# Pacing 2400 indirect DMAs on POOL: groups of eight behind a held no-op instead of groups of four with drains

## The reference, cut to what matters

```python
src = jnp.concatenate([edge_index[0], loops])
dst = jnp.concatenate([edge_index[1], loops])
e = jax.nn.leaky_relu(a_src[src] + a_dst[dst], negative_slope=0.2)
e_max = jax.ops.segment_max(e, dst, num_segments=M)
ee = jnp.exp(e - e_max[dst])
denom = jax.ops.segment_sum(ee, dst, num_segments=M)
alpha = ee / (denom[dst] + 1e-16)
msg = h[src] * alpha[:, :, None]
agg = jax.ops.segment_sum(msg, dst, num_segments=M).reshape(M, HEADS * NUM_EXPERTS) + b_gat
```

## Time and profile before

| what | us |
|---|---|
| median of 3 runs | 4237.11 |
| span of the profiled execution | 5018.1 |
| POOL busy in it | 2431.5 |
| DVE busy | 2254.2 |
| PE busy (matmul) | 2170.6 |
| ACT busy | 1178.5 |

### The profile page before, as it was taken

One profiled execution on the slowest core, in us unless ns is written; L12 is line 12 of the kernel. 1 busy time (PEld: TensorE's weight loads), 2 busy tenths in 40 slices (PEclk: granted clock), 3 DMA queues, 4 the chain that ended last, 5 costly groups with the idle time before them and its releaser, 6 DMA issues.

```text
span 5018.1 us, 28173 instructions
## 1 busy us (share of the span) xinstructions
PE 2170.6 (43%) x7631; PEld 912.4 (18%) x7631; DVE 2254.2 (45%) x3946; ACT 1178.5 (23%) x1734; POOL 2431.5 (48%) x2473
## 2 busy tenths in 40 slices
PE   0611278885456465556553143436564322000015
PEld 0211133332122121212111011112222111000014
DVE  8899867763336263635346531315140102101235
ACT  0300145552223232323222121224243312000001
POOL 0000162656653626161636666662636554777562
PEclk9955589987677676777766576678686656555557
DMA  3200044432223222322313221212122212011124
GB/s 87 39 1 0 21 73 76 74 71 46 37 52 65 37 61 46 64 41 46 61 19 68 35 49 28 56 34 63 41 68 55 64 34 87 10 24 22 31 47 145
DMA packets 652065, 247.84 MB, mean 49 GB/s; under 512 B 552276, under 2 KB 632708, under 8 KB 649476
## 3 DMA queue, kind: packets, MB, share of 16 engines
q1 hardware_dynamic: 573988, 216.76, 18.3%
q0 software_dynamic: 77920, 29.29, 5.8%
HBM read 152.68 MB, written 91.71 MB: 49 GB/s over the span
## 4 chain that ended last, share of the span: by engine, by line
PE 23%; another core or an unknown queue 20%; DVE 19%; issue 16%; POOL 8%; DVEq 7%; ACT 5%; DMA 2%; SPq 1%; ACTq 0%; POOLq 0%
POOL ring L790 8%; DVE res L1298 4%; PE ps L887 4%; DVEq L1300 4%; PE ps L877 2%; PE ps L991 2%; PE ps L902 2%; PE ps L1002 2%; PE ps L1013 1%; DVE res L1633 1%; DMA arena<-xnT 1%; PE ps L1052 1%; DVE arena L1659 1%; PE ps L950 1%
## 5 line engine op out<-in xcount | busy, mean ns | idle before, releaser
L790 POOL DMA_INDIRECT ring<-table,src_i x2048 | 2004.7, 979 | 1587.0 <-issue 883.0
L887 PE MATMUL ps<-arena,w 64*128 64x448 f32 x896 | 293.8, 740 | 441.5 <-issue 197.9
L754 POOL DMA_INDIRECT ring<-keys_d,place x128 | 138.8, 1084 | 653.8 <-DVEq L1255 589.5
L991 PE MATMUL ps<-arena 64*128 64x512 f32 x800 | 238.5, 710 | 360.2 <-DMA arena<-xnT 221.6
L1013 PE MATMUL ps<-ident,arena 128*128 128x128 f32 x800 | 156.1, 354 | 466.4 <-issue 272.7
L1805 DVE TENSOR_TENSOR arena<-ps,arena 128x1024 f32<-128x1024 f32 x68 | 83.3, 1225 | 594.9 <-remote 410.8
L902 PE MATMUL ps<-arena,w 128*64 128x448 f32 x896 | 247.7, 683 | 237.3 <-issue 237.3
L1645 DVE TENSOR_TENSOR arena<-arena,ps 128x448 f32<-128x448 f32 x297 | 174.8, 618 | 364.9 <-issue 195.7
L1186 ACT ACTIVATE arena<-ps,arena 128x1024 f32<-128x1024 f32 x200 | 217.0, 1115 | 256.6 <-remote 120.3
L1659 DVE TENSOR_TENSOR_SCAN arena<-ps,carry,arena 128x448 f32<-128x448 f32 x122 | 130.8, 1131 | 320.6 <-issue 178.0
L1105 ACT ACTIVATE ps<-ps,tb 128x448 f32<-128x448 f32 x297 | 171.9, 605 | 359.7 <-PE ps L887 154.9
(11 more groups left out here) (338 smaller groups left out, 3968.8 us busy)
## 6 DMA issues: line engine op xcount, KB each, us to landing
arena<-in_x SPq DMA_DIRECT2D x304, 110.0 KB
ring<-table,src_i POOLq DMA_INDIRECT x2048
partial<-res SPq DMA_DIRECT2D x15, 1536.0 KB
arena<-in_x SPq DMA_DIRECT2D x160, 140.0 KB
outputs_d<-arena SPq DMA_DIRECT2D x32, 512.0 KB
arena<-outputs_d SPq DMA_DIRECT2D x32, 512.0 KB
arena<-xnT SPq DMA_DIRECT2D x100, 128.0 KB
arena<-h_tok SPq DMA_DIRECT2D x50, 256.0 KB
```

The lines of the kernel that those rows point to most:

```text
L790: g.indirect_dma_start(out=ring[k % 2][:, j - FROM[k], :], out_offset=None, in_=table[0:GRAPH_NODES, :], in_offset=off(ap=src_i[:, j:j + 1 ...
L887: mm(bank(1 + (2 * i + z) % 3)[:, 0:CHUNK], w2[lower_upper(z), i * P:(i + 1) * P], h1[lower_upper(z), :], start=True, stop=True).then_inc( ...
L991: m = mm(hid[ee % 2][:, z * NT:(z + 1) * NT], fw1[lower_upper(z), ee, :], xf[q][lower_upper(z), :], start=True, stop=True)
```

## The change

`GROUP` becomes 8 and the drains go. The wait of each group is put on a no-op of its own that is not merged with the instruction behind it (`nofuse`), so that POOL's sequencer stands at it, and it waits for the group just in front, all eight, instead of the group two in front. It applies to the search, the scatters, all 2048 gathers and the nodes.

```diff
-GROUP = 4
-BURST = 16
-BURSTS_UNTIL = 1536
+GROUP = 8
...
-            def rest(n):
-
-                if n % BURST == BURST - 1 and n < BURSTS_UNTIL:
-                    g.drain()
+            def hold(done, value):
+
+                pool.wait_ge(done, value)
+                g.nop(nofuse=True)
 
             def group_landed(done, n):
 
-                if n % GROUP == 0 and n >= 2 * GROUP:
-                    m = n // GROUP
-                    pool.wait_ge(done[m % 2], 16 * GROUP * (m // 2))
-                return done[n // GROUP % 2]
+                m = n // GROUP
+                if n % GROUP == 0 and m:
+                    hold(done[1 - m % 2], 16 * GROUP * ((m + 1) // 2))
+                return done[m % 2]
 
             def node_group(n, j):
 
                 half = j // GROUP % 2
-                if j % GROUP == 0:
-                    of = n if j - 2 * GROUP >= NODE_BATCHES[n][0] else n - 1
-                    if of >= 0:
-                        pool.wait_ge(nrows[of % 2][half], node_count(of, half, j - GROUP))
+                if j % GROUP == 0 and j:
+                    of = n if j - GROUP >= NODE_BATCHES[n][0] else n - 1
+                    hold(nrows[of % 2][1 - half], node_count(of, 1 - half, j))
                 return nrows[n % 2][half]
 
             def gather_group(k, i):
 
-                half = i // GROUP % 2
-                if i % GROUP == 0 and i >= 2 * GROUP:
-                    pool.wait_ge(gath[k % 2][half], (gathered(k) - 16 * SIZES[k]) // 2 + 16 * (i // GROUP // 2 * GROUP))
-                elif i % GROUP == 0 and k:
-                    pool.wait_ge(gath[1 - k % 2][half], gathered(k - 1) // 2)
-                return gath[k % 2][half]
+                m = i // GROUP
+                if i % GROUP == 0 and i:
+                    hold(gath[k % 2][1 - m % 2], (gathered(k) - 16 * SIZES[k]) // 2 + 16 * GROUP * ((m + 1) // 2))
+                elif i == 0 and k:
+                    hold(gath[1 - k % 2][1], gathered(k - 1) // 2)
+                return gath[k % 2][m % 2]
...
             for k in range(P):
-                rest(k)
                 done = group_landed(search, k)
```

More of the change, by code:

```diff
@@ L771, in _ @@
                 for k in TILES_AFTER[j]:
-                    rest(n)
                     scatter(k, group_landed(scattered, n))
@@ L787, in _ @@
                 for j in range(FROM[k], FROM[k] + SIZES[k]):
-                    rest(j)
                     done = gather_group(k, j - FROM[k])
```

## The result

The changed kernel takes 4619.69 us (median of 4 runs, 4617.70 to 4623.08), the kernel before 4238.16 us beside it: 1.0895 times as long, with an interval of 1.0879 to 1.091. The forecast was 4356 us, the range ended at 4450 us. The sign is right and the size is not: +382 us instead of +119.

A forecast was written before the change was run, and what follows sets the result against it. It took the bound to change from stage to stage, with POOL's gathers setting the time from chunk 6 on. Its terms, 70 + 20 + 24 + 23 - 18 = +119 us, on 4237 gave 4356 us; range 4140 to 4450.

The forecast's parts named there:

- One hold: POOL standing at the no-op until the eight DMAs in front have landed: 1.5 us each, range 1.1 to 2.5.
- The end, chunks 13 to 16: Last gathers, with no drains to remove: 47 holds that count, at 1.5 us, +70 us (52 to 118).
- Chunk 12: Gathers of the chunk that had no drains: 16 holds, +24 us (18 to 40), counted for the timed runs.
- Chunks 6 to 11: Gathers taken as back to back: each loses 8 drains and gains 16 holds, together +23 us (-16 to +121).
- Chunks 0 to 5: First gathers: +3.8 us a chunk, taken as hidden by the waits for buffers, so nothing in the sum.
- Nodes: 128 gathers of nodes with 15 holds, 13 of them counted at 1.5 us: +20 us (0 to 33).
- Search and scatters: POOL's other DMAs: two holds' worth of cost each, taken as hidden, so nothing in the sum.
- Relief for PE: Front and experts: pauses twice as often halve the wait of PE's late semaphores, -18 us (-25 to 0).
- The faster rival: PE's late semaphores are in the timed runs and more frequent pauses relieve them: 4188 or 4118 us; chance 0.25.
- Only the end counts: POOL still waits for buffers in the middle, so chunks 6 to 12 are free: +72 us, 4309 us; chance 0.13.
- The missing hold: The no-op's wait does not stop POOL's stream, so drains go and nothing replaces them: 4116 us; chance 0.04.
- holds cheaper than any row: Holds at 0.81 us each bring the sum to zero, 4237 us; chance 0.08 together with the other even case.

The follow-up runs named there:

- e1: The kernel before with its drains taken out and nothing in their place: 3978.42 us, 0.937 times the kernel before.
- e5: The kernel before, unchanged, profiled once more: 4244.15 us, ratio 0.999, with a profiled span of 4245.1 us.
- e3: The changed kernel without the no-op, the same wait being carried by the group's first DMA: 4471.19 us, 1.0528 times the kernel before.
- e10: The changed kernel with holds in the nodes alone, nothing else paused: 3997.79 us, 0.9414 times the kernel before.
- e9: The changed kernel with holds in the search and the scatters alone, none in gathers or nodes: 4006.51 us, 0.944 times the kernel before.
- e2: The changed kernel without holds in chunks 12 to 16 and the nodes: 4460.88 us, 1.0502 times the kernel before.
- e4: The changed kernel with its held no-op kept, but waiting for the group two in front, no drains: 3970.03 us, 0.9345 times the kernel before.

## Why the prediction was wrong

*What bounds the kernel.* The prediction took POOL's busy stream for the bound, but "from number 6 on", with the holds of chunks 0 to 5 "hidden by the waits for buffers". That step failed. The cover, the 702.6 us of the earlier trace rows, exists only in the exceptional execution. In the timed kernel POOL streams from the first gather to the last, and the six chunks count like the others: they lost 96 us, where the sum had nothing and "up to +25 us" without the cover.

*The exceptional trace.* The argument from rates, 835 us lost under the profiler against 781 us of difference, led the right way: it said that the late semaphores have hardly any room in the timed runs, and e1 and e5 show none. What was not drawn from it is the plainer conclusion: a trace that is 18% longer than the runs shows another balance of stages, and slack in it is not slack. The Trainium skill ("NOTIFIC — the notification-queue block", section 7.1) was read as supporting a cause in the profiler. That rule may be right, but it does not explain why this one execution had late semaphores. The other eleven profiled executions, one of them of the same kernel, are each one of the timed runs as well, so a profiled execution is not as such a longer one. Idle time ended by "remote" adds up to 1380 us on ACT and 549 on DVE in the exceptional execution and to nothing in the eleven. No run here shows the cause.

*One hold.* This term was mis-sized: 1.5 us forecast, 2.25 measured on average (range given: 1.1 to 2.5). The working took DVE's 1.45 us from the earlier trace rows and set the issue behind the no-op off against the plain issue of 0.30. The landing of an undisturbed wait was about right: e3 has 1.69 us without other traffic, 1.39 more than plain issue. Two things were missing: the no-op adds 0.45 us beyond it, and waits beside SP's large transfers take longer, which raises the average by another 0.4. The Trainium skill ("DMA: Bandwidth & Descriptors", section Anatomy of one DMA — SWDGE (gpsimd) path) gives a DMA issued by POOL a fixed cost of about 2.0 us, by which, as an estimate, a hold would have been worth 0.75. The trace does not bear that out: in the timeline above the held group's first gather starts 3.01 us after the start of the one it waits for, 1.76 more than the 1.25 of an unheld one.

*The terms.* The end, chunks 13 to 16: +70 forecast, +102 measured. Chunk 12: +24, and +33.5. Chunks 6 to 11: +23, and +97. Chunks 0 to 5: 0, and +96. Nodes: +20, and e10 has 19 for their holds; the time behind the last gather's start grew by 22. Search and scatters: 0, and the first gather starts 22 us later; e9 has 28 more than without pauses, and the drains before had paid part of that. Relief for PE: -18, and there was nothing to relieve; the 50 us of lost PE time that it was taken from are in no run. With 2.25 us a hold, no cover and no relief, the prediction's own sum would be 106 + 29 + 36 + 95 + 95 + 32 = 393 us, 11 above the result. So of the 274 us that it lacked, 129 are the price of the 172 holds that it counted, 127 the holds of chunks 0 to 5, the search and the scatters that it took for hidden, and 18 the relief.

*The rivals.* The faster rival, with 0.25, fell with e1: without any pause the kernel is faster, not starved. "Only the end counts" fell with e2. The missing hold is excluded by the gaps in the timeline, and so are holds cheaper than any row. The rival that the prediction lacked is POOL's path from the first gather on. Its upper bounds, holds as dear as a drain from chunk 6 on, came to 4549 us; chunks 0 to 5 at that price, another 121, would have made it 4670. The range ended at 4450. The direction came out right, and for the stated reason: holds cost more than the drains they replace, and stand in the end, where there were none.

## What to carry to other kernels

Before a trace is costed, set its span beside the timed runs; where they differ by more than a few per cent, profile again, since slack read from such a trace may not exist. Where a queue's stream is the bound, every pause in it counts: here each drain cost 2.6 us and each hold on the group just in front 2.25 us, while a wait for a group two in front cost nothing that shows. Taking the drains out, with nothing else changed, made this kernel 6.3% faster (3978 us); with the no-op on the group two in front it was 6.5% (3970 us), which is not clearly better.

## What the runs showed of the hardware that was not expected

In one profiled execution of twelve, ACT started 15.7 us after the end of the PE group it waited for the earlier trace rows, and PE's rate was 0.64 matmuls a us beside a stream without drains. That a semaphore increment of PE arrived late is the reading of these rows. The same kernel profiled again, and kernels with more and with fewer pauses, had none of it. What set it off stays open.

A wait on a landing costs more in the stream than alone: 1.8 us on average beyond plain issue in e3, against 1.1 at the fix-up, and gaps of 4.5 to 7 us once in most chunks of the changed kernel, beside SP's large transfers. And a no-op that holds the sequencer costs 0.45 us when it has to wait and nothing that shows when its wait has already passed (e4).
